# Local attention plus top-2 experts on one core: values projected by row, copied into overlapping query blocks

## The reference, cut to what matters

```python
xn = layernorm(x)
qkv = xn @ w_qkv + b_qkv                       # q, k, v; 16 heads of 16
idx = arange(nw)[:, None] * 64 + arange(128)   # windows of 128 rows, one every 64
scores = einsum('bhnqd,bhnkd->bhnqk', q[idx], k[idx]) / 4
ow = einsum('bhnqk,bhnkd->bhnqd', softmax(scores), v[idx])
o = ow.reshape(b, nw * 128, c) @ w_out + b_out
attn = o[:, :512, :]
ffn = sum over the top 2 of 8 experts of p * (silu(xn @ w1) * (xn @ w2)) @ w3
out = x + attn + ffn
```

## Time and profile before

| | |
|---|---|
| median of 3 runs | 712.89 us (712.26 to 713.50) |
| the profiled execution | 713.24 us |
| its span, first to last instruction | 711.5 us |
| mean granted TensorE clock | 0.978 of full |
| TensorE busy | 633.2 us, 89% |
| VectorE busy | 571.6 us, 80% |
| ScalarE busy | 513.7 us, 72% |
| GpSimd busy | 280.4 us, 39% |

### The profile page before, as it was taken

The page is one execution under the profiler, slowest core; times in us unless marked ns, Lnnn a source line. Parts: engine busy times, 40 slices in busy tenths (PEclk is TensorE's granted clock), DMA queues, the critical chain, the costliest instruction groups (busy, mean ns, idle before and its releaser), DMA issues.

```text
span 711.5 us, 17988 instructions
## 1 busy us (share of the span) xinstructions
PE 633.2 (89%) x5916; PEld 512.0 (72%) x5917; DVE 571.6 (80%) x906; ACT 513.7 (72%) x883; POOL 280.4 (39%) x330
## 2 busy tenths in 40 slices
PE   0786776978999999999999999999889899999995
PEld 0564554754888888888888888888767676666673
DVE  4958899975688888888888888888687979788884
ACT  4554477474687787787777777777667788888885
POOL 3000273031344444444444444444300336666654
PEclk9998788998999999999999999999999999999999
DMA  9895477581111111111111111112168687885840
GB/s 300 268 257 174 128 262 273 146 284 31 49 53 52 59 52 52 59 53 50 59 55 50 57 56 51 56 54 56 45 161 258 174 259 180 271 227 161 215 138 30
DMA packets 66384, 92.74 MB, mean 130 GB/s; under 512 B 6448, under 2 KB 53424, under 8 KB 66320
## 3 DMA queue, kind: packets, MB, share of 16 engines
q1 hardware_dynamic: 57904, 70.56, 33.3%
q0 software_dynamic: 6864, 18.75, 7.9%
q10 hardware_dynamic: 1568, 2.76, 1.2%
HBM read 59.06 MB, written 32.83 MB: 129 GB/s over the span
## 4 chain that ended last, share of the span: by engine, by line
PE 63%; DVE 14%; ACT 10%; issue 8%; DMA 2%; POOL 2%; ACTq 0%; SPq 0%; DVEq 0%; POOLq 0%
PE PS L1300 55%; PE PS L1549 4%; DVE SMALL L964 4%; ACT WORK L781 3%; DVE XN L1122 2%; PE PS L1527 2%; DVE WALL L958 2%; ACT QS L776 1%; DMA XN<-in_x 1%; DVE WORK L1033 1%; DVE WORK L1026 1%; POOL OTS L595 1%; ACT WORK L719 1%; DVE WALL L982 1%; DMA KS<-parts_scratch 1%
## 5 line engine op out<-in xcount | busy, mean ns | idle before, releaser
L367 DVE TENSOR_TENSOR WS<-WALL,WS 128x1024 fp32r<-128x1024 f32 x136 | 166.9, 1227 | 56.0 <-ACT WS L862 41.5
L1300 PE MATMUL PS<-WS,XTS 128*128 128x512 f32 x804 | 203.9, 402 | 0.0
L1300 PEld LDWEIGHTS PS<-WS,XTS 128*128 128x128 f32 x804 | 146.2, 189 | 30.5
L862 ACT ACTIVATE WS<-WALL 128x1024 fp32r x136 | 143.7, 1056 | 9.1 <-issue 0.3
L1300 PE MATMUL PS<-DOWN_HIGH,HTS 128*128 x568 | 108.3, 290 | 5.0 <-DVE DOWN_LOW L958 3.5
L595 POOL TENSOR_TENSOR OTS<-SIDE,XN 128x256 f32<-128x256 f32 x31 | 23.8, 768 | 209.2 <-DVE XN L1122 142.2
L1300 PEld LDWEIGHTS PS<-DOWN_HIGH,HTS 128*128 128x128 f32 x568 | 86.4, 190 | 5.5 <-issue 5.5
L964 DVE TENSOR_REDUCE SMALL<-PS 128x8 f32<-128x1024 f32 x64 | 77.5, 1211 | 12.6 <-PE PS L1300 12.4
L781 ACT ACTIVATE WORK<-PS 128x512 f32<-128x512 f32 x128 | 69.4, 594 | 24.8 <-PE PS L1300 21.4
L658 POOL DMA_INDIRECT ys_scratch<-SIDE,SIDX x36 | 43.8, 1215 | 97.0 <-ACT SIDE L893 97.0
L654 POOL DMA_INDIRECT XS<-xn_scratch,GIDX x72 | 70.4, 978 | 23.6 <-issue 21.6
(11 more groups left out here) (148 smaller groups left out, 1094.8 us busy)
## 6 DMA issues: line engine op xcount, KB each, us to landing
WALL<-in_wexp SPq DMA_DIRECT2D x28, 384.0 KB, 7.1
WALL<-ys_scratch SPq DMA_DIRECT2D x16, 512.0 KB, 7.3
parts_scratch<-WORK SPq DMA_DIRECT2D x32, 240.0 KB, 2.5
QS<-parts_scratch SPq DMA_DIRECT2D x16, 480.0 KB, 4.6
XN<-in_x SPq DMA_DIRECT2D x4, 1024.0 KB, 12.1
xn_scratch<-XN SPq DMA_DIRECT2D x4, 1024.0 KB, 7.2
WALL<-in_x SPq DMA_DIRECT2D x8, 512.0 KB, 5.7
KS<-parts_scratch SPq DMA_DIRECT2D x16, 240.0 KB, 3.9
```

The costliest lines, as they stand in the source:

```text
L367: eng.tensor_tensor(out=WS[:, 1 - k, half, 1], in0=weights, in1=WS[:, 1 - k, half, 0].bitcast(F32), op=ALU.subtract).then_inc(low_ready[ha ...
L862: act.activation(WS[:, 1 - k, half, 0], weights, ACT.Copy).then_inc(high_ready[half], 1)
L1300: return pe.matmul(o, a, b, start=start, stop=stop)
```

## The change

Values are projected by blocks of 128 rows of the 320 (rows 0 to 127, 128 to 255, and the last 64), three projections instead of four. VTAKES lists the copies behind them. Each copy takes a range of partitions of the bank to the same partitions of a window. Windows 0 and 2 are whole blocks. Windows 1 and 3 start in the middle of a block, so that their upper 64 partitions hold the first 64 rows of the window, and the lower 64 the last 64: the halves stand exchanged. The turned scores of these odd windows, whose output partitions are the key rows, are therefore computed in two matmuls of 64 weight columns each, for every head. That makes six copies instead of four a batch: two in u = 4, none in u = 5, two in u = 6 and two in u = 7; and 16 matmuls instead of 8 in four units of a batch. Block 2 goes into 64 partitions of T_BANK, so that it need not wait until block 1 has left W_BANK. The next rows are loaded into XNT after seven projections instead of eight.

```diff
+VBLOCKS = -(-SPAN // P)
+BLOCK_USES = 4 + VBLOCKS
+VTAKES = (((0, 0, P), (1, STRIDE, P)), ((2, 0, P), (1, 0, STRIDE)), ((3, STRIDE, P),), ((3, 0, STRIDE),))
...
-                    sp.wait_ge(w_full, b * 8)
+                    sp.wait_ge(w_full, b * BLOCK_USES)
...
-            def take_values(n, bk, full, ready):
+            def take_values(i, bk, full, ready):
                 act.wait_ge(full[0], full[1])
-                act.activation(values_of(n), values_in(bk), ACT.Copy).then_inc(ready, 1)
+                for n, lo, hi in VTAKES[i]:
+                    last = act.activation(values_of(n)[lo:hi], values_in(bk)[lo:hi], ACT.Copy)
+                last.then_inc(ready, 1)
...
-                    for n in range(NWIN):
-                        take_values(n, FIRST_VALUES[n // 2][:, n % 2 * D:(n % 2 + 1) * D], (first_full, 6 + n // 2 * 2),
+                    for take, n in enumerate((0, 1, 1, 2)):
+                        take_values(take, FIRST_VALUES[n // 2][:, n % 2 * D:(n % 2 + 1) * D], (first_full, 6 + n // 2),
                                     values_taken)
...
-                    elif not last and u < UNITS - 1:
-                        take_values(u - 4, W_BANK[:, 0:D], (w_full, c["W"].add()), w_free)
+                    elif not last and u == 4:
+                        take_values(0, W_BANK[:, 0:D], (w_full, c["W"].add()), w_free)
+                    elif not last and u == UNITS - 2:
+                        take_values(1, W_BANK[:, 0:D], (w_full, c["W"].add()), block_taken)
...
                     if u == UNITS - 1 and not last:
-                        take_values(NWIN - 1, W_BANK[:, 0:D], (w_full, c["W"].add()), w_free)
+                        take_values(2, W_BANK[:, 0:D], (w_full, c["W"].now()), w_free)
+                        take_values(3, T_BANK[:, 0:D], (w_full, c["W"].add()), w_free)
...
             def project_values(o, n, xt, full):
+                rows = min(P, SPAN - n * P)
                 for ch in range(NC_D):
-                    last = mm(o, xt[:, ch, n * STRIDE:n * STRIDE + WIN], WQKV[:, ch, 2 * D:3 * D],
+                    last = mm(o[0:rows], xt[:, ch, n * P:n * P + rows], WQKV[:, ch, 2 * D:3 * D],
                               ch == 0, ch == NC_D - 1)
                 last.then_inc(full, 1)
...
             def values(n):
-                pe.wait_ge(w_free, c["W"].now() + 1)
-                project_values(W_BANK[:, 0:D], n, XNT, w_full)
+                last = n == VBLOCKS - 1
+                pe.wait_ge(w_free, c["W"].now() + (0 if last else 1))
+                project_values(T_BANK[:, 0:D] if last else W_BANK[:, 0:D], n, XNT, w_full)
                 c["W"].add()
...
-                        last = mm(o, KS[:, par, half * HH + h, w], QALL[0:DEEP, par, half * HH + h, w])
+                        moving = QALL[0:DEEP, par, half * HH + h, w]
+                        if n % 2 == 0:
+                            last = mm(o, KS[:, par, half * HH + h, w], moving)
+                        else:
+                            for part in range(2):
+                                at = (n + 1 - part) * STRIDE
+                                last = mm(o[part * STRIDE:(part + 1) * STRIDE],
+                                          KS[:, par, half * HH + h, at:at + STRIDE], moving)
...
-                        else:
+                        elif u < BLOCK_USES:
                             values(u - 4)
```

More of the change, by code:

```diff
@@ L312, in layer @@
         t_full, t_free = sem("t_full"), sem("t_free")
-        w_full, w_free = sem("w_full"), sem("w_free")
+        w_full, w_free, block_taken = sem("w_full"), sem("w_free"), sem("block_taken")
         s_full, s_free = sem("s_full"), sem("s_free")
@@ L1229, in batch @@
                 if not last:
-                    c["W"].add(NWIN)
+                    c["W"].add(VBLOCKS)
                 if ends(b):
@@ L1330, in gates @@
                 if b == 0:
-                    pe.wait_ge(values_taken, NWIN)
+                    pe.wait_ge(values_taken, len(VTAKES))
                 for ch in range(NC_D):
@@ L1351, in _ @@
                         project_block(FIRST_BANK[blk][:, 0:SPAN], blk, XT[0], first_full)
-                    for n in range(NWIN):
+                    for n in range(VBLOCKS):
                         project_values(FIRST_VALUES[n // 2][:, n % 2 * D:(n % 2 + 1) * D], n, XT[0], first_full)
```

## The result

| | before | changed |
|---|---|---|
| median | 712.94 us (712.26 to 713.50, 6 runs) | 716.81 us (715.47 to 719.07, 6 runs) |
| second measurement, other runs of both | 713.80 us (711.60 to 715.55, 22 runs) | 716.70 us (715.36 to 717.74, 5 runs) |
| the profiled execution | 713.24 us, span 711.5 | 719.07 us, span 717.3 |

The account below looks back on a forecast made before the run. TensorE was 89% busy, but ScalarE's strict row after u = 7 was taken to bound batches 3 to 6. Prologue -0.5, batches +0.15, -0.33, -0.04, +2.32, +0.15 summed to +1.75: 715.0 us, or 714.6 against the median; range 711.3 to 718.5.

Parts of the forecast that it names:

- rival A: Turned scores of odd blocks: half matmuls run one after another, +0.45 for +0.05 us, total 718.5 us; chance 0.15.
- prologue: Before the batches: one projection group less, -0.86, the narrow one +0.25, six copies beginning earlier; -0.5 us in all.
- batch 0: Copies of u = 5 and u = 7 on the chain, -0.28 and +0.28, and some of u = 6: +0.15 us.
- batches 3 to 6: Each pays 0.25 for the narrow projection, 0.05 for half matmuls, 0.28 for u = 7's second value copy: +2.32 us.
- The prediction's sign: Distance of the sums' reads in u = 7 between batches: longer by 0.58 us confirms the sum, shorter refutes it.
- drain: Narrow third projection in u = 6: changes of width drain TensorE and expose weight loads; 0.25 us, bounds 0 to 0.40.
- halves: Turned scores of odd blocks: 16 matmuls of 64 columns run side by side, costing +0.05 us over 8 whole ones.
- copy in u = 7: ScalarE's second value copy in u = 7 adds 0.28 us, on the path of batches 3 to 6.
- copies in u = 4 and 6: One more value copy in each; exponentials behind mostly wait for TensorE or have 0.6 us in hand: about 0.
- batches 1 and 2: Removing u = 7's projection gains 0.65 us, 0.32 after other costs; batch 1 -0.33, batch 2 -0.04 with its copy.
- Rival B: TensorE leads to the end of every batch, so the removed projection pays: 708.7 or 710.5 us, latter taken; chance 0.13.
- token load: Issued one unit earlier, after u = 6's third projection; its 1.1 us of waits disappear, worth 0, at best -0.3.

Follow-up runs that it names:

- halves_alone: The kernel before, with turned scores of odd windows made in two matmuls of 64 weight columns per head, keys in natural order; ratio 1.0016.
- whole_keys: The changed kernel with turned scores whole in all windows, so the key order of odd windows doesn't match their values; ratio 1.0044 against the kernel before.
- narrow_third: The kernel before, with only 64 rows of window 2 projected in u = 6, the other half of its values left stale; ratio 0.9997.
- no_values_u7: The kernel before without the value projection in u = 7; window 3 gets window 2's values, next rows loaded after seven projections; ratio 0.9998.
- no_projection_u6: The kernel before without the projection in u = 6; window 2 gets window 1's values, next rows loaded after seven projections; ratio 0.9968.
- third_full: The changed kernel with its third block at rows 192 to 319, full width, projected in u = 7; five copies; ratios 0.9973 and 0.9988 against the kernel before.
- copies_split_u4_u6: The kernel before with the copies of u = 4 and u = 6 split in two halves each, u = 7 left alone; ratio 1.0032.
- copy_split_u7: The kernel before with the copy of window 3 in u = 7 made in two halves of partitions, each behind its wait; ratio 1.0030.
- copy_split_no_wait: The kernel before with window 3's copy in u = 7 in two halves of partitions, one wait ahead of both; ratio 1.0022.
- third_spread: Against third_full: projections in u = 4, 6 and 7, and one copy in each of u = 4 and u = 5; ratio 0.9995 against the kernel before.

## Why the prediction was right or wrong

The direction held. The stated range, 711.3 to 718.5, held too, but by luck: its upper end was rival A's, and A's mechanism is not there. The forecast's own range, 713.2 to 715.9, missed the 716.8 and 716.7, and the size was +2.9 to +3.9 for +1.75. Term by term, the measured side from the table of the alignment:

| term | forecast | measured |
|---|---|---|
| prologue | -0.5 | -0.13 |
| batch 0, u = 3 to the next u = 1 | +0.15 | +0.4 (an estimate), +1.0 with the clock |
| batch 1 | -0.33 | +0.25 (0.68 with the wait of 0.36) |
| batch 2, to the next u = 1 | -0.04 | +0.65 (1.03 with the wait of 0.32) |
| batches 3 to 6 | +2.32 | +1.95 |
| batch 7 | +0.15 | +0.04 |
| sum | +1.75 | +3.1 |

The nearness of batches 3 to 6 is luck as well. The prediction's sign was the distance of the reads from batch to batch, 33.97 us longer by 0.58. It is longer by 0.48 in both executions of the changed kernel. But the 0.58 were 0.25 of drain, 0.05 of halves and 0.28 of copy. The 0.48 are 0.39 of copy in u = 7 and 0.10 of copies in u = 4 and 6, a term that the prediction put at nothing. In batches 4 to 6 drain and halves add nothing.

**The halves: right.** 0.56 for 0.55 us; `halves_alone` and `whole_keys` leave nothing in the batches behind the expert phase. Rival A, which wanted 1.0 us to the next group, fell. The Trainium skill (TensorE: Matmul & The Clock Gate, Part 3) says that weight loads overlap with matmuls in flight only when the row group differs; here the halves differ in their columns alone and 16 take no longer than 8, so the measurement decides.

**The drain: right in size, wrong in place.** It was to be 0.25 and on the path four times in batches 3 to 6. It measured 0.24; how much of that is a drain and how much a weight load in sight no run separates. But `narrow_third` has it in batches 1 and 2, a third of it in 3 and nothing in 4 to 6. There VectorE takes it up, between the maximum and the reciprocal. VectorE's timeline of `narrow_third` in batch 5, and GpSimd's at the same moment:

```profile
636.72 1.22 DVE L964 TENSOR_REDUCE SMALL<-PS 128x8 f32<-128x1024 f32 x1 [1.14 <-PE PS L1300]
637.98 0.39 DVE L1108 CAST MH<-SMALL 128x8 bf16<-128x8 f32 x1
638.40 0.17 DVE L958 TENSOR_TENSOR MH<-SMALL,MH 128x8 bf16<-128x8 f32 x1
638.49 1.75 DVE L1122 RECIPROCAL XN<-XN 128x256 f32<-128x256 f32 x1
```

```profile
637.62 0.73 POOL L603 TENSOR_TENSOR WALL<-WALL 128x256 f32<-128x256 f32 x1
```

The cast of 128 x 8 elements ends at 638.37, and the addition on GpSimd at 638.35. In the kernel before the same cast takes 0.64 and ends 0.02 behind the same addition:

```profile
641.78 0.64 DVE L1108 CAST MH<-SMALL 128x8 bf16<-128x8 f32 x1
```

```profile
641.67 0.73 POOL L603 TENSOR_TENSOR WALL<-WALL 128x256 f32<-128x256 f32 x1
```

So `narrow_third` moved the start of the cast by 0.25 us, and its end not at all: the cast is 0.25 shorter instead. The reciprocal starts when GpSimd's addition is over, whether the maximum came 0.25 later or not. GpSimd's row there is fed by ScalarE's scalings. That step of the prediction read the chain as TensorE's scores, maximum, reciprocal, division, and missed that the middle of it was stretched by an engine which the chain doesn't name.

**The copy in u = 7: on the path as forecast, with the wrong price and one place too few.** 0.39 for 0.28. The two halves of window 3 start at different partitions, and the row that the term was priced by has both copies at partition 0. Five boundaries pay it, not four: in batch 2 the prediction had set the copy against a gain that isn't there. 5 x 0.39 = 1.95 is half to two thirds of the whole.

**Batches 1 and 2: wrong.** Here the step from "a closed row of TensorE work" to a gain of 0.65 failed. The row has no idle time, but the read of the sums depends on two things, and the division was as late as TensorE's group. GpSimd's timeline of the kernel before, batch 2:

```profile
543.14 0.73 POOL L595 TENSOR_TENSOR OTS<-SIDE,XN 128x256 f32<-128x256 f32 x1 [6.58 <-DVE XN L1122]
```

It ends at 543.87, and the read starts at 543.97. `no_values_u7` gave 0.00 for the 0.65 that I had counted. With the gain gone, the drain stays: +0.25 in each, and in batch 2 the copy.

**The copies in u = 4 and u = 6: counted at nothing, cost 0.10 a batch in 4 to 6.** Two in u = 4 and none in u = 5 leave +0.13. The second in u = 6 leaves -0.03, because there is slack behind it in short steps: the scalings to the next exponentials take 0.80 (610.92 to 611.72) where they took 1.00 in the kernel before (607.11 to 608.11).

**The prologue: right in kind, too large.** TensorE's timeline of the changed kernel (answers to the earlier trace rows) and ScalarE's (to the earlier trace rows):

```profile
31.25 2.90 PE L1308 MATMUL PS<-WQKV,WALL 128*128 128x256 f32 x12
34.08 1.10 PE L1332 MATMUL PS<-IDF,XN 128*128 128x128 f32 x8
35.57 0.64 PE L1308 MATMUL PS<-WALL 128*32 128x128 f32 x16 [0.40 <-ACT VW L747]
```

```profile
33.18 2.25 ACT L747 ACTIVATE VW<-PS 128x256 f32<-128x256 f32 x6 [1.20 <-PE PS L1308]
```

The values take 2.83 us for 3.45, as forecast. But the six copies take 2.25 (I had 1.78), and the gate matmuls wait 0.40 for them. Four of the five steps from one copy to the next change the start partition here; 4 x 0.39 + 0.28 + 0.38 for the last is 2.22. From the start of the values to the gates it is 4.32 for 4.45.

**Rival B** was wrong for u = 7 and not wholly wrong as a mechanism: TensorE's time ahead of the scores of u = 6 does count. A projection less there gives 0.14 to 0.40 in five batches of six (`no_projection_u6`), and `third_full` gains in batches 2 and 3. The change spends time there (0.24) and saves it behind them.

**The token load**: its waits were to go. They went from three to one, of 1.1 us as the three together, and a new one appeared, TensorE behind the last copy. The waits of the changed kernel from 514 us on: us, times, longest (answers to the earlier trace rows):

```profile
PE PS L1308 <- ACT VW L747: 2.5, 4, 0.7
...
PEld PS L1308 <- DMA WORK<-xt_scratch: 1.1, 1, 1.1
```

**Batch 0: the copies and the clock.** Between the reads of u = 5 and u = 7 the changed kernel adds 1.06, far more than its second copy is worth. TensorE's timelines of the kernel before and of the changed kernel show the projection of u = 6 there:

```profile
98.08 1.03 PE L1300 MATMUL PS<-WQKV,WORK 128*128 128x256 f32 x4
```

```profile
98.31 1.97 PE L1308 MATMUL PS<-WQKV,WORK 128*64 128x256 f32 x4
100.21 1.03 PE L1308 MATMUL PS<-KS,QS 96*128 96x128 bf16 x8
```

In the changed kernel it falls into a stretch of half clock (98.2 to 101.6, granted clock 0.50), and ScalarE's exponentials behind it wait 0.87 us for TensorE:

```profile
102.82 1.08 ACT L786 ACTIVATE WORK<-PS 128x512 f32<-128x512 f32 x2 [0.87 <-PE PS L1308]
```

The 13 traces beside that of the kernel before sort by this:

| traces | projection of u = 6, clock | copies in u = 6 | added, 0, 5 to 0, 7 |
|---|---|---|---|
| narrow_third | 1.08 us, full | 1 | +0.02 |
| copies_split_u4_u6 | 1.03 us, full | 2 | +0.33 |
| halves_alone, copy_split_u7, no_values_u7, copy_split_no_wait | 1.91 us, half | 1 | +0.59 to +0.66 |
| changed (two), whole_keys | 1.79 to 1.97 us, half | 2 | +1.06 to +1.14 |
| third_spread | 1.91 us, half, in a longer stretch (5.0 us for 3.4) | 2 | +1.35 |
| no_projection_u6 | none | 1 | +0.01 |
| third_full (two) | none | 2 | +0.07 and +0.10 |

So some 0.6 of the 1.06 come with the clock, 0.33 with a second copy, and the rest, 0.1, fits the narrow projection at half clock. The two steps around it are as forecast in kind: -0.29 up to u = 5, where the copy of u = 5 is gone (-0.28), and +0.20 to the next u = 1 for the second copy of u = 7 (+0.28). Without the clock batch 0 costs -0.29 + 0.46 + 0.20 = +0.4, an estimate from these rows. With this +0.4 the sum of the table is +3.1, between the two measurements (2.9 and 3.9). The prediction had left about 1 us for the clock, and that is what the two differ by.

**What stays open** is why the clock falls where it does, the prologue's spread, and the small term of batch 3 (+0.12 from u = 1 to u = 7, where drain, copies and waits shift against each other).

## What to carry to other kernels

Before counting a removed instruction as a gain, go to the next instruction that joins two engines and ask when its *other* input was ready; a row without idle time says that an engine is busy, not that it is last. Price an added instruction by a row with the same partitions as well as the same shape, and count every place where it stands in a strict row. When values are shared between overlapping blocks, lay the blocks so that the copy at the batch boundary stays a single one: the third block at rows 192 to 319 removes one projection as well, and pays none of the 0.39. And line traces up by a recurring instruction, with the granted clock of each stretch beside them, before a difference of whole times is put down to the change.

## What the runs showed of the hardware

- **ScalarE and start partitions.** A copy of 128 or 64 partitions with 256 elements takes 0.38 us. A copy that starts at the same partition as the one ahead of it starts 0.28 us behind it (610.37 to 610.92: 0.55 for a pair and the step to what follows). When one starts at 64 and the other at 0, the second starts 0.40 behind (581.10 to 581.50), when the first has ended, and costs 0.39. With what follows at partition 0 again the pair of u = 4 takes 0.80 for 0.55.
- **VectorE behind GpSimd.** From 514 us on the kernel before has 45 casts of 128 x 8. 26 of them take 0.17 us. The other 19 take 0.24 to 0.73, and each of these ends 0.02 to 0.03 us behind the end of a GpSimd addition that runs beside it. `narrow_third` moved the start of one by 0.25, and its end stayed. The Trainium skill (GPSIMD Engine Reference, Specifications) says that GpSimd shares its interfaces with VectorE, with contention in some of VectorE's modes; the coincidence fits that, but no experiment moved GpSimd's addition alone, so the cause is argued and not shown.
- **Two column groups of 64 run side by side.** 16 matmuls of 64 weight columns take 0.56 us where 8 of 128 take 0.55.
- **The granted clock.** The same four fp32 matmul records of an output projection take 1.10 us at full clock and 2.04 at half. Batches 0 and 1, where TensorE waits 1 to 2 us in a unit for ScalarE (2.00 ahead of the scores at 96.49, before the fall at 98.2), have stretches of half clock. From 177 to 705 us there are none in any trace. Where they lie can differ between two executions of the same kernel: `third_full` has one from 65.6 to 69.0 us, its repetition from 55.8 to 62.7.
